# Four edits around layer 1 of a two-layer cross-attention and FFN kernel: order of a loop, who computes two kinds of roots, an earlier place list, and idle matrix turns at both ends

## The reference

```python
x = x + L0_xattn(_layernorm(x), ctx)          # 16 heads of 64, projections Wq Wk Wv Wo
x = x + L0_ffn(_layernorm(x))                 # a shared FFN, and one of two experts per token (top 1)
x = x + L1_xattn(_layernorm(x), ctx, ctx)     # one head: softmax(x' ctx^T / 16, masked) ctx
x = x + L1_ffn(_layernorm(x))                 # x' quantised to int8 by one scale for all tokens
                                              # (largest |x'| of all), int8 product, scaled back, bias

def _layernorm(x, eps=1e-5): return (x - mean(x)) / sqrt(var(x) + eps)
```

## Time and profile before

| | |
|---|---|
| three runs | 934.39, 936.97, 938.98 us; median 936.97 |
| the profiled execution | 934.39 us in all; its span, first to last instruction, is 932.6 us |
| TensorE busy | 891.0 us (96% of the span) |
| VectorE busy | 604.3 us (65%) |
| ScalarE busy | 530.8 us (57%) |
| GpSimd busy | 257.6 us (28%) |
| the chain that ended last | TensorE 90%, VectorE 6%, ScalarE 1%, DMA 1% |
| mean granted clock of TensorE | 0.989 of full speed |

### The profile page before, as it was taken

The page is one execution under the profiler, slowest core; times in us unless marked ns, Lnnn a source line. Parts: engine busy times, 40 slices in busy tenths (PEclk is TensorE's granted clock), DMA queues, the critical chain, the costliest instruction groups (busy, mean ns, idle before and its releaser), DMA issues.

```text
span 932.6 us, 19542 instructions
## 1 busy us (share of the span) xinstructions
PE 891.0 (96%) x6634; PEld 781.4 (84%) x6634; DVE 604.3 (65%) x1653; ACT 530.8 (57%) x1267; POOL 257.6 (28%) x325
## 2 busy tenths in 40 slices
PE   5999999999999999999999999999989999999884
PEld 4788888998888888899888898887878999997553
DVE  6578666666656666666765666666644666348876
ACT  4665655566655665556655565655742555457645
POOL 1343243333423434333342343333100000042000
PEclk9999999999999999999999999999989999999997
DMA  9402000000000000000000000000441142265502
GB/s 283 123 8 108 1 23 18 6 16 5 21 16 5 16 5 18 20 5 16 5 21 8 13 16 6 1 7 11 155 151 53 44 169 92 76 174 165 164 27 79
DMA packets 29502, 50.23 MB, mean 54 GB/s; under 512 B 2961, under 2 KB 24113, under 8 KB 27681
## 3 DMA queue, kind: packets, MB, share of 16 engines
q1 hardware_dynamic: 27920, 45.97, 15.9%
q0 software_dynamic: 1536, 3.67, 1.3%
HBM read 41.37 MB, written 8.26 MB: 53 GB/s over the span
## 4 chain that ended last, share of the span: by engine, by line
PE 90%; DVE 6%; ACT 1%; issue 1%; DMA 1%; POOL 0%; SPq 0%; POOLq 0%; DVEq 0%
PE bank L1798 27%; PE bank L1827 10%; PE bank L1955 9%; PE bank L2043 9%; PE bank L1846 8%; PE bank L1812 8%; PE bank L1867 5%; PE bank L1771 4%; PE bank L2131 2%; PE bank L2149 2%; PE bank L1780 1%; DVE neg_max L1238 1%; PE bank L2007 1%; DMA stage<-in_wk 1%; PE bank L1744 1%
## 5 line engine op out<-in xcount | busy, mean ns | idle before, releaser
L758 POOL TENSOR_TENSOR probs<-probs,row_rcp 112x375 f32<-112x375 f32 x256 | 209.4, 841 | 389.3 <-DVE row_rcp L1244 387.7
L863 ACT ACTIVATE probs<-bank,neg_max 112x375 f32<-112x375 f32 x256 | 144.5, 570 | 56.3 <-DVE neg_max L1238 56.1
L1827 PE MATMUL bank<-ident,probs 112*125 112x112 f32 x768 | 129.2, 278 | 4.0 <-DVE probs_t L1249 4.0
L1827 PEld LDWEIGHTS bank<-ident,probs 112*125 112x125 f32 x768 | 113.3, 187 | 21.2 <-issue 6.2
L1238 DVE TENSOR_REDUCE neg_max<-bank 112x1 f32<-112x375 f32 x256 | 123.2, 539 | 11.1 <-PE bank L1812 10.9
L1249 DVE COPY probs_t<-bank 125x336 f32<-125x336 f32 x128 | 64.7, 507 | 61.0 <-PE bank L1827 57.0
L835 ACT ACTIVATE k_parts<-bank 128x376 fp32r<-128x376 f32 x128 | 62.1, 485 | 66.1 <-PE bank L1798 66.1
L1798 PE MATMUL bank<-ctx_hi,down_hi 128*128 128x376 f32 x256 | 96.3, 376 | 0.8 <-DVE q_parts L1225 0.6
L838 ACT ACTIVATE v<-bank 125x512 f32<-125x512 f32 x96 | 57.5, 599 | 65.0 <-PE bank L1798 65.0
L1229 DVE TENSOR_TENSOR k_parts<-bank,k_parts 128x376 fp32r<-128x376 f32 x128 | 69.8, 546 | 29.0 <-ACT k_parts L835 28.0
L1846 PE MATMUL bank<-probs_t,v 125*64 125x112 f32 x1536 | 87.7, 263 | 0.0
(11 more groups left out here) (226 smaller groups left out, 1978.3 us busy)
## 6 DMA issues: line engine op xcount, KB each, us to landing
ctx_raw<-in_ctx_t SPq DMA_DIRECT2D x16, 375.0 KB, 3.4
stage<-in_ffn_up SPq DMA_DIRECT2D x5, 1024.0 KB, 5.2
stage<-in_ffn_down SPq DMA_DIRECT2D x5, 1024.0 KB, 6.8
ring_late<-in_ctx_t SPq DMA_DIRECT2D x10, 375.0 KB, 10.4
ring_late<-in_ctx_n SPq DMA_DIRECT2D x10, 375.0 KB
routed<-xn SPq DMA_DIRECT2D x1, 2240.0 KB, 9.5
rows_in<-routed SPq DMA_DIRECT2D x5, 448.0 KB, 6.3
answers<-y_rows SPq DMA_DIRECT2D x10, 224.0 KB, 2.9
```

Of the source, the lines that this page charges most:

```text
L758: eng.tensor_tensor(probs[s][:, :], probs[s][:, :], row_rcp[:, s:s + 1].broadcast_to([S, C]), ALU.mult).then_inc(probs_ready, 1)
L863: eng.activation(probs[r][:, :], SCORE_BANKS[i][0:S, 0:C], ACT.Exp, bias=neg_max[:, r:r + 1], accum_out=row_sum[:, r:r + 1]).then_inc(exp_ ...
L1827: t = eng.transpose(turn_bank(i, project)[0:CJ, j * S:(j + 1) * S], probs[QUAD * v + i][:, j * CJ:(j + 1) * CJ], ident[0:S, 0:S])
```

## The change

- **Opening, TensorE.** As soon as the identity is there, 24 turns of the identity matrix by itself, into a bank that nobody reads yet (`turn_identity(24, TURN_BANK)`). After the last `mix_context` of layer 1, 60 more.
- **End of layer 0 attention.** All thirteen `norm_op` of the last two batches stand in stage 2 (before: seven in stage 2, six in 3); normalising and choosing stand in stage 3 (before 4), the turning and counting on TensorE in stage 4 (before 5), the copies of ScalarE in stage 5 (before 6), and the places in stage 4 (before 6).
- **Third norm.** It has a column of its own for each batch (in the tiles of the first norm). Of groups 2 and 3 VectorE computes only the first four operations; the three Newton steps and the shift are done by GpSimd, fourteen operations a group, behind its gathers. Groups 0 and 1 stay with VectorE, a stage sooner or later. `normalise_group` is cut in two halves of two batches.
- **Layer 1 loop.** `masked(t + 1)` stands behind `soft(t)` on ScalarE, and `largest(t + 1)` ahead of `update(t - 2)` on VectorE: each one batch ahead of where it was. The largest and smallest elements are reduced for two batches at a time.
- **Fourth norm.** ScalarE computes sqrt(var + eps), for batches 0 to 11 first and for 12 to 15 when they are there; VectorE takes the reciprocal (one operation in place of thirteen).

```diff
@@ gpsimd
+            for g in range(POOL_ROOTS, NG):
+                cols = slice(GB * g, GB * g + GB)
+                half, term, rstd = (t[:, cols] for t in (norm3.half, norm3.term, norm3.rstd))
+                base = 14 * (g - POOL_ROOTS)
+                eng.wait_ge(norm3.step, (2 * GB + NORM_OPS) * POOL_ROOTS + (2 * GB + SEED_OPS) * (g - POOL_ROOTS + 1))
+                for i in range(3):
+                    if i:
+                        eng.wait_ge(root_step, base + 4 * i)
+                    eng.tensor_tensor(term, rstd, rstd, ALU.mult).then_inc(root_step, 1)
...
+                eng.tensor_scalar(shift3[:, cols], term, -1.0, None, ALU.mult).then_inc(root_step, 1)
@@ scalar
-            def normalise_group(g):
-
-                eng.wait_ge(norm3_ready, g + 1)
+            def normalise_group(g, h):
+
+                if g < POOL_ROOTS:
+                    eng.wait_ge(norm3_ready, g + 1)
+                else:
+                    eng.wait_ge(root_step, 14 * (g - POOL_ROOTS + 1))
...
-                    if s == 0 and m == 6:
+                    if s == 0 and m == 5:
                         for j in range(2):
                             tokens_out(1, B - 2 + j, bank[6][:, KT * S * j:KT * S * (j + 1)])
...
+            masked(0)
             for t in range(B):
-                masked(t)
                 if t >= 1:
                     attn_out(t - 1)
                 soft(t)
-                if t % GB == 1 and t // GB + 1 < NG:
-                    normalise_group(t // GB + 1)
                 if t % GB == 2 and t // GB + 1 < NG:
                     group_out(t // GB + 1)
+                if t + 1 < B:
+                    masked(t + 1)
+                if t % GB < 2 and t // GB + 1 < NG:
+                    normalise_group(t // GB + 1, t % GB)
             attn_out(B - 1)
+            eng.wait_ge(abs_zeroed, 2)
+            for cols in (slice(0, B - 4), slice(B - 4, B)):
+                eng.wait_ge(norm4.step, min(2 * cols.stop + 1, 2 * B))
+                eng.activation(norm4.var[:, cols], norm4.moments[:, cols, 1], ACT.Sqrt, bias=eps_col[0:S, 0:1]) \
+                   .then_inc(root_ready, 1)
@@ vector
                     if s == NS - 1:
+                        if m == 2:
+                            norm3_merge(0)
                         if m == 3:
-                            norm3_merge(0)
                             norm3_stats(0)
                             norm3_moments(0)
-                            norm3_ops(0, 0, 5)
                         if m == 4:
-                            norm3_ops(0, 5, NORM_OPS)
-                        if m == 5:
+                            norm3_ops(0, 0, NORM_OPS)
+                        if m == 6:
                             norm3_merge(1)
...
+            largest(0)
             for t in range(B + 2):
-                if t < B:
-                    largest(t)
+                if t + 1 < B:
+                    largest(t + 1)
...
+                if t == 0:
+                    norm3_merge(2)
+                    norm3_stats(2)
+                if t == 1:
+                    norm3_moments(2)
+                    norm3_ops(2, 0, SEED_OPS)
+                if t == 3:
+                    norm3_merge(3)
...
-            eng.wait_ge(norm4.step, 2 * B)
-            for i in range(NORM_OPS):
-                norm_op(norm4, 2 * B, i, slice(0, B))
...
+            largest_x(B - 1, 1, 0)
+            largest_x(B - 1, 1, 1)
+            eng.wait_ge(root_ready, 2)
+            eng.reciprocal(norm4.rstd, norm4.var[:, :]).then_inc(norm4.step, 1)
@@ tensor
+            def turn_identity(times, psum):
+
+                for _ in range(times):
+                    eng.transpose(psum[:, 0:P], ident[:, :], ident[:, :])
+
             eng.wait_ge(consts, 2)
+            turn_identity(24, TURN_BANK)
             turn_tokens(0, 0, heads_bank[0])
...
-                        if m == 5:
+                        if m == 4:
                             for j in range(2):
                                 turn_tokens(1, B - 2 + j, bank[6][:, KT * S * j:KT * S * (j + 1)], xn[1 - j])
...
             mix_context(B - 1)
+            turn_identity(60, GROUP_BANKS[0])
```

126 lines of the change are left out of this document (69 added, 57 removed).

## The result

| | before | after |
|---|---|---|
| median of 7 runs | 936.97 us (934.21 to 938.98) | 930.90 us (927.31 to 931.94) |
| ratio, 95% interval | | 0.9936 (0.9919 to 0.9953) |
| the profiled execution, its span | 932.6 us | 929.0 us |
| forecast | | 930.4 us (926.0 to 934.5) |

What follows compares the result with a forecast made beforehand. TensorE, busy 891.0 of 932.6 us, was taken as the bound. Terms 0 + 0.5 + 0 - 0.1 - 4.7 - 2.0 - 0.4, rounded to -6.6, took the median 936.97 to 930.4 us, range 926.0 to 934.5.

Steps and rivals of the forecast that it cites:

- The loop, and its remainder: Layer 1 loop: TensorE's last product 6.1 us sooner, 1.4 lost to VectorE's later last moments, so -4.7 us.
- The signs that it named: Layer 1 loop: no TensorE wait above 0.3 us after batch 4, last product at about 900.
- the second rival: First batches of the layer 1 loop: late heads of queues cost 1 to 3 us, giving 932 to 933; chance 18%.
- GpSimd being too slow: Third norm's Newton steps on GpSimd delay TensorE: 938.4 us (6%), or 931 to 936 in a milder case (12%).
- The root: Fourth norm, last moments to the product with the root: 3.13 us becomes 1.13, so -2.0 us.
- Segment 0: First FFN segment: the block of the last two batches takes TensorE 2.10 us, +0.5 us.
- Segment 1: Turning of the rows: the 3.15 us stall stays because y_update(0) ends it; 0 us.
- The last segment: Last FFN segment: merge and norm of group 0 stand a stage sooner, no TensorE wait for them; -0.1 us.
- The opening and layer 0: Opening: the 24 turns of the identity cost nothing and give 0 us, with a gain of 0.4 as the far end.
- The turns at the end: Behind the layer 1 loop: sixty turns may hold TensorE's clock, given one half; -0.4 us, between 0 and 0.9.

Runs made afterwards that it cites:

- e2: The changed kernel with the Newton steps of groups 2 and 3 back on VectorE: 930.37 us, ratio 0.9932 to the kernel before.
- e9: The changed kernel with the layer 1 loop in its former order, GpSimd's Newton steps kept: 934.05 us, ratio 0.9983 to the kernel before.
- e3: The changed kernel with the fourth norm's root back on VectorE, thirteen operations: 931.15 us, ratio 0.9933 to the kernel before.
- e5: The changed kernel with the last two batches' norm, choice, turning, copies and places in their former stages: 928.88 us, ratio 0.9934 to the kernel before.
- e10: The changed kernel with GpSimd's first bias addition made to wait until VectorE has written q_parts: 927.23 us, ratio 0.9923 to the kernel before.
- e1: The changed kernel without the sixty turns of the identity behind the layer 1 loop: 929.89 us, ratio 0.9918 to the kernel before.
- e4: The changed kernel with 74 turns behind the loop instead of 60, and more in TensorE's two rests: 927.78 us, ratio 0.9897 to the kernel before.
- the last two kernels: The changed kernel with several follow-up edits together, 925.47 us, and the same without any turns of the identity, 926.94 us.

## Why the prediction was right, and where it was not

**The loop, and its remainder.** Forecast 6.1 us less at TensorE and 1.4 of it lost to VectorE's backlog; measured 6.11 and 1.13. Laying the new order out by durations from the trace gave this. The signs that it named came too: no wait of TensorE behind the first one (0.71 us, forecast 0.86), and the last product ends 50.99 us after the first energies, where 51.2 were forecast. Of the late heads of queues in the second rival nothing shows. What the text said of the reason was half right: it named the Newton steps and the order in one breath. e2 and e9 show that the order does it. The chance of 18 in 100 for GpSimd being too slow was spent on an edit of 0.2 us.

**The root.** Forecast 3.13 to 1.13 us, measured 1.03. That the 2.1 us reach the end in the mean is not shown (e3).

**Segment 0.** Forecast +0.5, measured +0.45, and 0.52 by e5. TensorE idles 0.34 us for `xn`, for which it had not waited before, and the same 0.72 us for the choice. The 1.5 us that the clock took there in three other profiles was in no term.

**Segment 1.** Forecast: the stall stays. It did, in before, after and e5. The forecast overlooked that behind this wait the clock fell or did not, and for 6.83 or 3.41 us: 10.29, 7.66 and 9.22 us behind it with nothing changed there. I had the larger of these in hand (it is in the profiled execution) and took it for fixed.

**The last segment.** Forecast -0.1; measured +0.66 in this pair, -0.2 in seven of twelve profiles. The five others are those with a pause of ScalarE, below.

**The opening and layer 0.** Forecast 0, measured 1.8 us in this pair: 0.7 from the landing of `x_all`, some 0.5 from GpSimd's addition beside VectorE, 0.45 unexplained. None of it was a term of the sum or a rival.

**The turns at the end.** This is the step that failed, the -0.4. It rests on "If it holds, the turns and products of the first group are 0.3 to 0.9 us shorter", and that came true: in the changed kernel they are 0.35 and 0.68 us shorter (0.55 for 0.90, 1.02 for 1.70). What was wrong is that this would reach the end. The integers wait for VectorE all the same, and the forecast looked only at the gap ahead of the first of them (2.1 us forecast, 1.63 measured) and not at the rests behind, of 1.11 and 0.43 us in the timeline of before, which a faster TensorE made longer (1.46 and 1.32). In this profile the clock's fall was put off from where no work was into the second group's products, and the tail grew by 2.1 us.

**The sum.** From the profiled pair it would be 3.6 us, not 6.6. The medians give 6.1. The parts that repeat are -6.11 + 1.13 - 2.10 + 0.45 (segment 0) + 0.45 (layer 0), and with the uncertain 0.6 of the turns they make -5.6 us; the forecast of -6.6 was right to 1 us because its errors are small beside the loop, and to 0.5 us by chance.

## What to carry to other kernels

When an engine waits for an in-order queue, moving a result one turn ahead of its use can be worth more than taking operations out of the queue: here, with the order unchanged, the next operation was late in their place. Work put in to keep a clock up is to be judged where the clock is needed: sixty turns that ended ahead of the work kept it up through the tail in two profiles of eight and in others moved the slow stretch into the work; with the rests filled too it stayed up in two of two. One profile of a kernel is one draw where the clock may fall: read a second before a difference there is given to an edit. Before hastening what a wait seems to be about, look which instruction ends as the wait ends: here the addition and not the rows, and moving that one by a stage was worth 2.2 us of wait, and 1.6 to 2.6 more where the clock had fallen behind it.

## What the runs showed of the hardware

**GpSimd and VectorE.** In ten profiles (all nine of changed kernels without the added wait, and the second one of before) a VectorE operation of 112x3 with two operands in SBUF takes 0.58 to 0.74 us in place of 0.16, and ends within 0.03 us of GpSimd's 112x256 addition; beside `q_parts`, which reads a PSUM bank, the same addition held up nothing. The Trainium skill (SBUF — State Buffer, "SBUF: two separate sides") says that the two share a port pair as an exclusive lock, that whichever starts first keeps it, and that a VectorE operation with two SBUF inputs is of those that need it. The trace agrees: in all ten GpSimd's addition starts first, and in e10 the same addition, begun 0.23 us ahead of `wv_lo`, makes it 0.38 us longer. I had used the rule only in one direction, VectorE holding up GpSimd's steps, which cost one step 0.16 us; it was GpSimd that held up VectorE.

**Pauses that no instruction explains.** In five of the twelve profiles of changed kernels ScalarE stops around the copy of the last expert's answers, and the `relu` behind it starts 2.6 to 2.9 us late. In the changed kernel the stop stands ahead of the copy:

```profile
833.24 1.16 ACT L1015 ACTIVATE y_t<-bank,b_part 128x448 f32<-128x448 f32 x2 [2.37 <-remote]
```

The profile calls the releaser "remote". In the four others (e1 to e4) ScalarE waits 1.0 to 1.1 us ahead of the copy and 1.7 to 2.0 behind it, in e1 so:

```profile
836.21 0.63 ACT L1043 ACTIVATE hid<-bank,b_col 128x448 f32<-128x448 f32 x1 [1.97 <-PE bank L2000]
```

TensorE's products are on time there. VectorE's share of group 0's norm is then late, and TensorE waits 0.65 to 0.81 us for the second half of the normalised rows. GpSimd's 10.54 us in the last two kernels have no releaser either. An instruction load lands near the place of ScalarE's pause, but it does so in all fourteen profiles (5.5 to 6.1 us into the last segment), with the pause and without. The cause of both is open.
